# Row maxima of the second attention from stacks of their own, in pairs on row halves of TensorE

## The reference, cut to what matters

```python
q, k, v = split(x @ W_qkv + b_qkv)            # 16 heads, D = 8 features each
alibi  = minimum(idx[None, :] - idx[:, None], 0)
scores = einsum('bhtd,bhsd->bhts', q, k) / sqrt(D) + slopes[:, None, None] * alibi
w = softmax(scores, axis=-1)
y = einsum('bhts,bhsd->bhtd', w, v)           # then @ W_proj + b_proj, and added to x
```

## Time and profile before

| | us |
|---|---|
| median of 3 runs | 1325.85 |
| the profiled execution | 1338.45 |
| span of its trace | 1336.7 |
| second attention, from its first DMA issue to the next block | 690.15 to 1157.16 |
| its chunks before the first score | 720.13 to 749.13 |
| mean granted TensorE clock | 0.925 |

### The profile page before, as it was taken

One profiled execution on the slowest core, in us unless ns is written; L12 is line 12 of the kernel. 1 busy time (PEld: TensorE's weight loads), 2 busy tenths in 40 slices (PEclk: granted clock), 3 DMA queues, 4 the chain that ended last, 5 costly groups with the idle time before them and its releaser, 6 DMA issues. The chain is left out here.

```text
span 1336.7 us, 18924 instructions
## 1 busy us (share of the span) xinstructions
PE 1179.0 (88%) x6275; PEld 584.1 (44%) x6275; DVE 845.3 (63%) x1874; ACT 705.9 (53%) x883; POOL 520.2 (39%) x540
## 2 busy tenths in 40 slices
PE   4899999999999977679857999999999999777885
PEld 2444444444444953469722222223222223446774
DVE  6366666666656467623337988888888884584232
ACT  3678777777778153022223466666666667421221
POOL 0066566665657103268600111311321321035774
PEclk9899999999999978789967799999999999697898
DMA  2000100100101106147544402022022000313662
GB/s 81 1 6 24 33 22 22 32 22 22 38 17 33 34 1 193 21 110 189 98 101 93 94 1 48 2 48 49 1 49 48 1 2 1 117 46 70 147 179 22
DMA packets 59211, 70.75 MB, mean 53 GB/s; under 512 B 21354, under 2 KB 45806, under 8 KB 58478
## 3 DMA queue, kind: packets, MB, share of 16 engines
q1 hardware_dynamic: 44956, 60.76, 17.5%
q0 software_dynamic: 11264, 8.92, 4.7%
q10 hardware_dynamic: 2920, 0.16, 0.1%
HBM read 50.25 MB, written 9.83 MB: 45 GB/s over the span
## 5 line engine op out<-in xcount | busy, mean ns | idle before, releaser
L1675 DVE TENSOR_REDUCE at_MX<-psum 128x1 f32<-128x512 f32 x512 | 318.1, 682 | 54.0 <-PE psum L1808 54.0
L1625 ACT ACTIVATE at_PR<-psum 128x1024 f32<-128x1024 f32 x256 | 251.5, 1022 | 164.6 <-PE psum L1823 163.5
L1808 PE MATMUL psum<-at_KS,at_QS 120*128 120x512 bf16 x512 | 205.3, 403 | 7.7 <-DMA at_KS<-at_SPL 6.7
L1562 POOL TENSOR_TENSOR at_PR<-at_PR,at_FAC 128x512 f32<-128x512 f32 x64 | 81.0, 1266 | 329.6 <-ACT at_PR L1625 329.6
L1823 PE MATMUL psum<-at_QS,at_KS 122*128 122x512 bf16 x512 | 191.8, 385 | 0.8 <-DMA at_QS<-at_MR 0.3
L478 ACT ACTIVATE PR<-psum 128x1024 f32<-128x1024 f32 x144 | 141.0, 1027 | 82.1 <-PE psum L762 74.0
L483 ACT ACTIVATE PR<-PR 128x1024 f32<-128x1024 f32 x144 | 144.5, 1062 | 0.0
L762 PE MATMUL psum<-Q,K 64*128 64x512 f32 (+3 forms) x768 | 143.5, 502 | 1.2 <-ACT PR L478 1.2
L1839 PE MATMUL psum<-at_PR,at_VG 128*32 128x512 f32 x1024 | 136.2, 604 | 8.4 <-ACT at_OTS L1618 4.5
L774 PE MATMUL psum<-PR,V 128*64 128x512 f32 (+3 forms) x768 | 139.7, 495 | 0.1
L1330 PE MATMUL psum<-moe_XGT,moe_WE 128*128 128x256 f32 x512 | 125.6, 402 | 7.5 <-ACT moe_XGT L1089 7.5
(11 more groups left out here) (223 smaller groups left out, 1566.6 us busy)
## 6 DMA issues: line engine op xcount, KB each, us to landing
moe_WE<-in_c_We SPq DMA_DIRECT2D x32, 768.0 KB
XB<-at_r_dram SPq DMA_DIRECT2D x32, 256.0 KB, 3.9
at_QS<-at_SPL SPq DMA_DIRECT2D x72, 64.0 KB
at_KS<-at_SPL SPq DMA_DIRECT2D x72, 64.0 KB
at_KS<-in_c_krows SPq DMA_DIRECT2D x8, 384.0 KB
moe_rows_dram<-XNS SPq DMA_DIRECT2D x2, 1152.0 KB, 11.5
at_QS<-at_MR SPq DMA_DIRECT2D x124, 1.0 KB
Wqkv<-in_c_Wqkv SPq DMA_DIRECT2D x8, 192.0 KB
```

What stands on the lines that cost most here:

```text
L1562: pool.tensor_tensor(pr, pr, FAC[:, 4 * (s // 2):4 * (s // 2) + 4, :], ALU.mult).then_inc(z.factored, 1)
L1625: act.activation(PR[:, gu % PRS, 2 * r:2 * r + 2, :].rearrange("p h n -> p (h n)"), g.psum[:, 2 * r * BANK:(2 * r + 2) * BANK], ACT.Exp).t ...
L1675: dve.tensor_reduce(MX[:, 4 * (r // 2 % 4) + r // 8, r % 2:r % 2 + 1], bank(("max", c))[:, :], AX, ALU.max).then_inc(z.reduced, 1)
L1808: pe.matmul(bank(("max", c))[:, :], QS[0:MROW, t, h, I * P:(I + 1) * P], KS[0:MROW, t, h, khalf * BANK:(khalf + 1) * BANK], start=True, st ...
```

## The change

The maxima pass gets stacks of its own, `QM` and `KM`, with two parts instead of three: four products of 8 rows and 32 bias rows, 64 rows a head (`MROWS`). Two heads stand in one stack, one on partitions 0 to 63 and one on 64 to 127, and `max_pair` issues two matmuls, one for each head on its half of the array's rows, into two ring banks. Only the second tells VectorE. The stacks of the values pass stay as they are, but two copies remain (`STACKS` = 2) of both kinds. TensorE's round is now four scores, a pair, the values, a pair. `turn_maxima` and `split_maxima` move from behind chunk 1 to behind chunk 3 of the next half (`ROW_AT`). `take` moves ahead of both exponentials of its unit. SyncE issues 16 or 18 DMAs more a step.

```diff
-STACKS = 3
+STACKS = 2
+MPARTS = 2
+MPRODUCTS = MPARTS * MPARTS * DH1
+MROWS = MPRODUCTS + MPARTS * 2 * BT
+MSTACK_DMAS, MSTACK_FIRST = 2 + 4 * MPARTS * MPARTS, 2
+ROW_AT = 3
...
-        if c % 32 == 1 and 32 < c < CHUNKS1 + 2:
+        if c % 32 == ROW_AT and 32 < c < CHUNKS1 + 4:
...
+                def max_part_rows(s):
...
+            for k, ready in enumerate((y.high, y.mid)):
+                for side, into in enumerate((QM, KM)):
+                    for r in range(MPARTS):
+                        for h in range(2):
+                            row = 64 * h + DH1 * product
+                            sp.dma_start(into[row:row + DH1, t, :, :], SPL[q + QUADS * h::2 * QUADS, n, k, :]
+                                         ).then_inc(z.mstacks[t], 16)
...
                 for hs in range(HALVES):
-                    s = hs // 2 + 2
+                    s = hs // 2 + 1
                     maxima_rows(sp, hs, 0)
                     if hs:
                         maxima_rows(sp, hs, 1)
+                    if hs % 2 == 0:
+                        wait(sp, z.maxed, 32 * (s - 1))
+                        if s > 1:
+                            max_bias_rows(s)
+                        max_part_rows(s)
+                    else:
+                        wait(sp, z.scored, 2 * UNITS * (s - 1))
                         bias_rows(s)
                         part_rows(s)
...
+                    if gu % BT == 2 and gu > BT:
+                        take(gu // BT - 1)
                     for r in range(2):
                         act.wait_ge(z.scored, 2 * gu + r + 1)
...
-                        if r == 0 and gu % BT == 2 and gu > BT:
-                            take(gu // BT - 1)
...
+                def max_pair(c):
+                    for h in range(2):
+                        ring_free(("max", c + h))
+                    for h in range(2):
+                        rows = slice(64 * h, 64 * h + MROWS)
+                        mm = pe.matmul(bank(("max", c + h))[:, :], QM[rows, t, pair, I * P:(I + 1) * P],
+                                       KM[rows, t, pair, khalf * BANK:(khalf + 1) * BANK], start=True, stop=True)
+                    mm.then_inc(z.maxed, 1)
...
                 for gu in range(last + 1):
-                    for h in range(4):
-                        if gu < last:
+                    if gu < last:
+                        for h in range(4):
                             score_head(gu + 1, h)
-                        turn(4 * (gu + LEAD) + h)
+                    turn(4 * (gu + LEAD))
+                    if gu:
+                        multiply(gu - 1)
+                    turn(4 * (gu + LEAD) + 2)
                     if gu % BT == 2 and gu > BT:
                         turn_out(gu // BT - 1)
-                    if gu:
-                        multiply(gu - 1)
```

More of the change, by code:

```diff
@@ L1421, in stage_alibi_attention @@
     z.stacks = [sem(f"at1_stacks{t}") for t in range(STACKS)]
+    z.mstacks = [sem(f"at1_mstacks{t}") for t in range(STACKS)]
     with ExitStack() as tmp:
@@ L1431, in stage_alibi_attention @@
         KS, QS = sb("KS", [P, STACKS, 4, SEQ], BF16), sb("QS", [P, STACKS, 4, SEQ], BF16)
+        KM, QM = sb("KM", [P, STACKS, 2, SEQ], BF16), sb("QM", [P, STACKS, 2, SEQ], BF16)
         FAC = sb("FAC", [P, H1, P])
@@ L1465, in chunk @@
             hs, k = c // 32, c % 32
-            return hs // 2, hs // 2 % STACKS, (k // 2) % 4, 4 * (hs % 2) + k // 8, k % 2
+            return hs // 2, hs // 2 % STACKS, (k // 4) % 2, 4 * (hs % 2) + k // 8, (k // 2) % 2
         def maxima_rows(eng, hs, k):
@@ L1509, in _ @@
                 sp.dma_start(bv[:, :], g.i["c_bv"].partition_broadcast(P)).then_inc(y.loaded, 16)
+                max_first_rows(0)
+                max_bias_rows(0)
                 first_rows(0)
@@ L1513, in _ @@
                 sp.dma_start(HB[:, :], g.i["c_bproj"].partition_broadcast(P)).then_inc(y.out, 16)
+                max_part_rows(0)
                 part_rows(0)
[L1515 to L1518, removed]
+                max_first_rows(1)
+                max_bias_rows(1)
                 sp.dma_start(FAC[:, :, :], g.i["c_factor"]).then_inc(z.factors, 16)
-                first_rows(2)
-                bias_rows(2)
                 for hs in range(HALVES):
-                    s = hs // 2 + 2
+                    s = hs // 2 + 1
                     maxima_rows(sp, hs, 0)
@@ L1526, in _ @@
                         maxima_rows(sp, hs, 1)
[L1527 to L1531, removed]
+                    if s == STEPS1:
+                        continue
+                    if hs % 2 == 0:
[5 more added lines that the diff above has]
+                        wait(sp, z.scored, 2 * UNITS * (s - 1))
+                        if s == 1:
+                            first_rows(1)
                         bias_rows(s)
@@ L1672, in reduce_chunk @@
                 def reduce_chunk(c):
-                    dve.wait_ge(z.maxed, c + 1)
-                    r = c % 32
-                    dve.tensor_reduce(MX[:, 4 * (r // 2 % 4) + r // 8, r % 2:r % 2 + 1], bank(("max", c))[:, :], AX,
+                    dve.wait_ge(z.maxed, c // 2 + 1)
+                    _, _, pair, I, khalf = chunk(c)
+                    dve.tensor_reduce(MX[:, 4 * (2 * pair + c % 2) + I % 4, khalf:khalf + 1], bank(("max", c))[:, :], AX,
                                       ALU.max).then_inc(z.reduced, 1)
@@ L1802, in ring_free @@
                         pe.wait_ge({"max": z.reduced, "row": z.msplit, "out": z.normed}[kind], i + 1)
[L1804 to L1809, removed]
+                def max_pair(c):
+                    s, t, pair, I, khalf = chunk(c)
+                    for h in range(2):
+                        ring_free(("max", c + h))
+                    for h in range(2):
+                        rows = slice(64 * h, 64 * h + MROWS)
+                        mm = pe.matmul(bank(("max", c + h))[:, :], QM[rows, t, pair, I * P:(I + 1) * P],
+                                       KM[rows, t, pair, khalf * BANK:(khalf + 1) * BANK], start=True, stop=True)
+                    mm.then_inc(z.maxed, 1)
                 def turn_maxima(hs):
@@ L1819, in score_head @@
                     if h == 0 and gu % BT == 0:
+                        if gu % UNITS == 0:
+                            pe.wait_ge(z.stacks[t], 16 * (STACK_FIRST + STACK_DMAS * (s // STACKS + 1)))
                         pe.wait_ge(z.mrows, 128 * (gu // BT) + 128)
@@ L1853, in turn @@
                             s = c // 64
-                            pe.wait_ge(z.stacks[s % STACKS], 16 * (STACK_FIRST + STACK_DMAS * (s // STACKS + 1)))
-                        max_chunk(c)
-                    if c % 32 == 1 and 32 < c < CHUNKS1 + 2:
+                            pe.wait_ge(z.mstacks[s % STACKS], 16 * (MSTACK_FIRST + MSTACK_DMAS * (s // STACKS + 1)))
+                        max_pair(c)
+                    if (c + 1) % 32 == ROW_AT and 32 < c < CHUNKS1 + 4:
                         turn_maxima(c // 32 - 1)
@@ L1886, in _ @@
                 pe.wait_ge(y.out, 32)
-                for c in range(4 * LEAD):
+                for c in range(0, 4 * LEAD, 2):
                     turn(c)
@@ L2036, in arrays @@
     a["c_mones"] = np.ones([2, 4 * SEQ], HOST_BF16)
+    a["c_max_krows"] = np.ascontiguousarray(
+        np.concatenate(krows[:MPARTS], 1).reshape(QUADS, MROWS - MPRODUCTS, 2, 2, SEQ).transpose(0, 3, 1, 2, 4)
+        .reshape(QUADS, 2, MROWS - MPRODUCTS, 2 * SEQ))
     a["c_krows"] = np.ascontiguousarray(np.concatenate(krows, 1).reshape(QUADS, -1, 4 * SEQ))
```

13 lines of the change are left out of this document (added).

## The result

The changed kernel takes 1332.67 us, the median of 5 runs (1332.21 to 1333.54), against 1325.85 us of the kernel before (5 runs beside it, 1324.57 to 1327.19): 6.8 us more, a ratio of 1.0052 with a 95% interval of 1.0035 to 1.0069. The forecast was 1340 with a range of 1314 to 1361; the direction holds, the size is half.

The account below looks back on a forecast made before the run. TensorE was taken to set the pace in the middle of the block. Halves -3, clock falls +15 and the start +2 gave +14 us on 1325.85, so 1340 us, with a range of 1314 to 1361.

Parts of the forecast that it names:

- The round: TensorE's scores, pairs, values and four changes of array shape: 2.63 us forecast, against 2.85 before.
- pairs one behind the other: Rival: a pair's two matmuls run in series, round 3.05 us, total 1367 us; chance 0.10.
- The trip: Maxima rows through SyncE's eight small DMAs, from split to the score that needs them: 5.95 to 6.05 us.
- The wait: TensorE waits 2.4 us in each half for the maxima rows, where it waited for nothing before.
- The removed stall of the negation: The negation lasted 0.79 us over GpSimd's factor in some halves; coming later in its round saves 0.25 a half.
- the 0.6 of the take: Time TensorE's values wait behind each take, saved by moving it ahead of both exponentials: 0.6 us a half.
- The stacks: Rival: new stacks' DMAs come late, 3 us of wait in 7 steps, 1361 us; chance 0.08.
- the clock term: TensorE's clock falls to 0.50 for 3.41 us behind 9 of 15 waits, 1.7 us lost each: +15 us.
- one row and the two bounds: Another block's clock fall behind 1.87 us idle, and none or all of 15 halves falling: 0 and +26 us.
- the start: Ahead of the first score: 3.4 us earlier start, 24 pairs each 0.16 short, later clock rise; +2 us net.
- The clock holds: Rival: the wait is there but TensorE's clock stays at 1.00; 1320 to 1332 us; chance 0.24.
- The trip stays hidden: Rival: maxima rows land in time, halves of 22.3 us, -35 us, 1291 us; the faster case, chance 0.12.

Follow-up runs that it names:

- e_one: Changed kernel with the negative maximum in one bf16 row instead of two, so four small DMAs a half instead of eight: 1299.57 us, ratio 0.972 to the kernel before.
- e_lead13: Changed kernel with the maxima 13 units ahead instead of 12, a round more between split and score: 1306.24 us, ratio 0.9761 to the kernel before.
- e_before_take: Kernel before with only the take moved ahead of both exponentials: 1327.29 us, ratio 0.9921 to the kernel before.
- e_fill: Changed kernel with ten score matmuls nobody reads ahead of each half's wait for the maxima rows: 1333.22 us, ratio 0.9969 to the kernel before.
- e_take: Changed kernel with the take put back between the two exponentials of its unit: 1366.56 us, ratio 1.0208 to the kernel before.
- e_row1: Changed kernel with maxima turned and split behind chunks 0 and 1 of the next half instead of 2 and 3: 1316.16 us, ratio 0.9841 to the kernel before.

## Why the prediction was half right

**What held.** The round: 2.63 forecast, 2.61 measured; the two matmuls of a pair start 3 to 6 ns apart, so "pairs one behind the other" is out. The trip: 6.05 us at most, 6.08 to 6.16 measured in halves 1 to 14. The wait: 2.4 us forecast, and the half is 2.2 longer than without it (24.63 less 22.44); that the first weight load is idle for 2.4 too is partly luck, since 0.23 of it stands in every round. The half without the trip: 22.3, and 22.44 in e_one and 22.47 in e_lead13. The half with it: 24.7, and 24.63. The removed stall of the negation (0.79 to 0.17) and the 0.6 of the take (e_before_take). The stacks were not late: their issues end long before the first score of a step. That makes the stretch from half 0 to half 15 without falls 3.6 us shorter (1.3 + 6.0 less 7 falls x 1.55), for a forecast of -3.

**The step that failed** is the size of the clock term: "I take 9 of them", at 1.7 us, "+15 us". It holds 4 of the 8 us by which the block's +5.7 falls short of +14; the start and the end, below, hold the others. The mechanism is as told (e_fill: without the idle time no fall, and everything else unchanged), but there are 7 falls, and one costs 1.55 us (26.18 less 24.63), so +10.9; e_fill, without them, takes 10.5 us less from the split of half 0 to that of half 15. The count had no better ground than one row and the two bounds; e_take shows that it can't be had from the length of the wait alone: the same idle time of 2.12 to 2.19 us lowers the clock at 7 of 14 halves in changed and at 13 of 14 in e_take. The row itself is no firmer: at the place of the earlier trace rows the trace of the changed kernel has an idle time of 1.83 us ahead of 45.97, and the clock stays at 1.00 from 43.23 to 50.06. And the trace of the kernel before had more places to count: behind TensorE's idle times at full clock that end at 545.89 (2.41 us) and 706.23 (1.79 us) the clock stays at 1.00 for 2 us and more, behind the one that ends at 1199.23 (2.41 us) it falls at 1200.3. That nine was near seven is luck in part.

The page that I had weighed against the earlier trace rows, of the Trainium skill, "TensorE: Matmul & The Clock Gate", section "Why this matters for your kernels", lets only longer idle gaps lower the clock. By it the term would be 0, and the block would have come out 3.6 us shorter in its middle. The trace disagrees: 2.14 us of idle TensorE at 910.46 to 912.60, and the clock at 0.50 from 913.6; the same at seven waits of 2.12 to 2.16 us. The 0.8 to 1.4 us of e_row1 never did it.

**The start and the end.** I had +2 for the start; it is +0.1, by larger terms than mine on both sides. The first chunk starts 6.1 us earlier (3.4 forecast). Ahead of the first score 24 pairs take 6.2 us more than 48 chunks, 0.26 each (0.16 forecast): at half clock the pairs start 1.49 us apart (703.91, 705.40), of which VectorE's two reductions take 1.29 and its wait for the next pair 0.20. At the end the last half and what follows it are 1.6 us shorter, which I had left out. The last half is 0.6 shorter by the take: with the take moved alone (e_before_take) it is 22.61 us, with the take put back (e_take) 23.29, against 22.65 and 23.25. The 1.0 behind the last values goes with the clock there: 14.77 us at a mean clock of 0.72 before, 13.78 at 0.84 with the change, 12.54 at 0.96 in e_one and e_before_take. The change has no work in that stretch, so this part of the forecast's miss was chance. So 0.1 + 10.9 - 3.6 - 1.6 = +5.8 us, against the block's +5.7 and 6.8 in the times.

**The rivals.** "The clock holds" would have been -5.1 by these numbers (5.8 less 10.9); e_fill, which makes it nearly true, has a block 2.0 us shorter than before. "The trip stays hidden" was priced at -35; e_one, which makes it true, has a block of 429.4, 37.7 us shorter than before.

## What to carry to other kernels

When a change makes the rounds of a loop shorter, look for the round trips that run beside a fixed number of them: what was hidden with half a us to spare turns into the bound, and takes the whole gain (2.2 us a half here). Cut the trip (fewer issues) or give it more rounds before cutting rounds. On TensorE a wait has a second price: behind an idle time of 2.1 us the clock went to half for 3.4 us in half of the cases here, and in nearly all when the halves were longer (e_take), and work that nobody reads, put into the wait, can be worth its place (e_fill).

## What the runs showed of the hardware

- Idle times of 2.12 to 2.19 us of TensorE, one in each half, lowered its clock at 7 of 14 halves, the same ones in a second trace, and at 13 of 14 in e_take. Each fall began between 0.3 us ahead of the end of the idle time and 1.6 behind it. Idle times of 0.8 to 1.4 us (e_row1) never did. One place of another block had 1.87 us with a fall in one trace and 1.83 without in the other. What decides among equal waits stays open.
- Ahead of the first score TensorE works at half clock for 35 us (715 to 750 in e_one), busy for 15.39 of them; when useless pairs made it 23.82 of 35, the mean clock was 0.95.
- A small operation of VectorE on SBUF (the negation, 128 x 16) takes 0.17 us, and took 0.79 where it ran over a GpSimd multiplication. In the changed kernel it starts 0.3 us behind the end of that multiplication (929.52, for 929.19). In e_lead13 it runs over GpSimd again in four halves and takes 0.92 to 0.93.
- Two bf16 matmuls of 64 rows on the two halves of the array's rows start 3 to 6 ns apart: the pair is 0.32 us from its start to the next instruction (908.75 to 909.07), some 0.1 of it for the change of shape by the 0.09 of the earlier trace rows.
